# A pipelined transformer block on one core: a new slot table for the feed-forward tiles, and projections on two PSUM banks

## The chip, the cores and the metric

The kernel runs on 1 core of one Trainium2 chip. The metric is the device time of one execution in microseconds, as the median of several runs. Each run stands alone; nothing is averaged over cores.

## What is computed

The reference takes x (16 x 512 x 256, float32) and computes

```python
x = x + 0.5 * ffn(layernorm(x))
x = x + attn(layernorm(x))
x = x + 0.5 * ffn(layernorm(x))
```

`attn` has 16 heads of 16. Of each row of 512 scores only those at or above the 31st largest stay, the others go to -inf before the softmax:

```python
scores = einsum('bhqd,bhkd->bhqk', Q, K) / sqrt(16)
thresh = top_k(scores, 31)[0][..., -1:]
scores = where(scores < thresh, -inf, scores)
context = einsum('bhqk,bhkd->bhqd', softmax(scores), V)
```

`ffn` is a mixture of 16 attention experts with shared weights of the gate in both uses. The gate gives each token 16 weights rw (normalised logits against sim_matrix, relu, a fall-back to the best two, softmax); q, k and v are sums over the experts of rw times a 256 x 64 projection; then one causal attention with head size 64, and an output projection of each expert weighted by rw again.

## The kernel before

All arithmetic is float32. The work is cut into tiles of 128 tokens, 64 in all, 4 to a batch of 512. Two jobs walk over the tiles: job b is the first feed-forward layer (load of x, layer norm, gate, experts, attention, y, second layer norm, xnT), job a is the output projection of the attention and then the second feed-forward layer, with the store. Between them stands the big attention: for each batch 64 units (16 heads x 4 tiles of queries), each 128 queries x 512 keys.

**The order is written by hand, as a table of slots.** A batch has SPAN = 64 slots. For every slot each engine's program issues what the tables name, in order of slots; nothing else schedules. A unit of the attention takes one slot: the scores of a quad of four units (SC, slot 4c + 2, L482), their eviction from PSUM into the ring S of 16 units (EV, 4c + 3, ACT L705), the search of pairs of units by MAX8 and MATCH_REPLACE8 (TOP, 2p + 4, VectorE L812, L814), the threshold as a bias (NBI, POOL L945), ReLU (ACT L716), subtraction (SUB, POOL L950), Exp (ACT L721), transposes (TR, L514), eviction (PTE, L711), PV (L538), and a transpose and copy into ctxr (CT, CTT, CTX). A search of a pair is 14 instructions; it is the work of VectorE.

**The feed-forward tiles** have a slot for every step in AT["a"] and AT["b"], one tile every TILE = 16 slots. Attention of batch n has slots 64n on; job b works ahead of it and job a behind it. Steps named later: x_sum, x_mean, x_sq, x_rstd, h, hT, h_rinv, lg (the front: layer norm, transpose, logits of the gate), shift, top, pair, repl, gate, gate_exp, gate_em, gate_sum, rw, rwT, rw_st (the 16 gate rows, stored to rows_a or rows_b in DRAM), hs (four chunks of four experts: rows are read back, spread over 128 partitions into RB, and POOL multiplies, HS = hT x RB, L909; TensorE then adds the group into pQ, L497), qkv, qkT, sc, sc_max, sc_nmax, sc_exp, sc_rec, sc_norm, pT, attT (the causal attention), rb2 and mix (L927, attT times gate rows), y (L442 and L446, output projection in two halves, then the residual). Job a begins with ctx_rec (VectorE L781), ctx_norm (POOL L851) and ctxT (TensorE L376, left by ACT L617).

**Banks.** Each job has one PSUM bank F (pFa, pFb). Every fill waits until the fill before it has been read (`read`), counted by `fill()` from the table FILLS. The six projections Q0, K0, V0, V1, Q1, K1 of a batch (L466, L473) fill bank b; ACT leaves them to QT, KT and Vst, and VMOVE copies Vst into V. HS and RB have two buffers each and are shared by the jobs; RB2 and mixT have one.

**Queues.** SyncE issues all DMAs in slot order and waits before each for what it needs: x_ld, rw_st, four loads of RB, two of RB2, out. The weights of the attention come in `late_loads()` within the slots of tile 0.

Jobs and attention share VectorE, ACT, POOL and TensorE, so an engine that waits in one step holds up all that stands behind it in the table. `earlier()` and `due()` work out from the tables how many events lie before a slot:

```python
def due(w, j, slot, period, total):
    if (j - slot) % period:
        return None
    k, c = SPAN // period, (j - slot) // period
```

Of the kernel before, what the change touches and what calls it, by code (L numbers as in the profile page):

```python
# [5 lines left out]
F32 = mybir.dt.float32  # L6
# [38 lines left out]
    "a": {k: v - 2 * TILE for k, v in {  # L45
        "ctx_rec": 69, "ctx_norm": 71, "ctxT": 72, "x": 74, "x_mean": 75, "x_sq": 76, "x_rstd": 77, "h": 78,
        "hT": 79, "h_rinv": 79, "lg": 81, "shift": 82, "top": 83, "pair": 84, "repl": 85, "gate": 87,
        "gate_exp": 88, "gate_em": 89, "gate_sum": 90, "rw": 91, "rwT": 92, "rw_st": 93, "hs": 96, "qkv": 104,
        "qkT": 105, "sc": 107, "sc_max": 107, "sc_nmax": 109, "sc_exp": 110, "sc_rec": 111, "sc_norm": 112,
        "pT": 114, "rb2": 110, "attT": 116, "mix": 117, "y": 119, "out": 120,  # L50
    }.items()},
    "b": {k: v - SPAN for k, v in {
        "x_ld": -51, "x_sum": -48, "x_mean": -47, "x_sq": -46, "x_rstd": -45, "h": -44, "hT": -43, "h_rinv": -43,
        "lg": -41, "shift": -40, "top": -39, "pair": -38, "repl": -37, "gate": -34, "gate_exp": -33,
        "gate_em": -32, "gate_sum": -31, "rw": -30, "rwT": -29, "rw_st": -28, "hs": -24, "qkv": -16, "qkT": -15,
        "sc": -14, "sc_max": -13, "sc_nmax": -11, "sc_exp": -10, "sc_rec": -9, "sc_norm": -8, "pT": -6,
        "rb2": -10, "attT": -4, "mix": -3, "y": 0, "y_mean": 2, "y_sq": 3, "y_rstd": 4, "y_norm": 5, "xn": 8,
# [941 lines left out]
```

## Time and profile before

| | us |
|---|---|
| median of 3 runs (4930.96 to 4932.72) | 4932.21 |
| the profiled execution, its own time | 4928.01 |
| its span, first to last instruction | 4926.2 |
| busy: VectorE 92%, TensorE 81%, POOL 75%, ACT 69% | 4551.2, 4014.7, 3710.7, 3383.5 |
| granted TensorE clock, mean over the span | 0.915 of 2.4 GHz |

A "busy" share is taken over the whole span and over stages with different limits. The matmuls' ends are modelled, so busy TensorE is not TensorE at its peak. The durations of single instructions overlap by some tenths of a microsecond when they run back to back, so the distance from start to start is shorter than the duration.

### The profile page before, as it was taken

What the parts mean: (1) busy time and instruction counts of PE and PEld (TensorE: products, weight loads), DVE (VectorE), ACT (ScalarE), POOL (GpSimd) and SP (SyncE); (2) the same over time, 40 slices, a digit from 0 to 9 for tenths busy, and PEclk for the clock granted to TensorE, in tenths of its full rate; (3) what the DMA queues carried; (4) which work ended last, traced back from release to release, by engine and by line L of the source; (5) the groups of instructions that cost most, each with busy time, mean ns of one, the idle gap of its engine ahead of it and who ended that gap; (6) DMA issues with size and microseconds to landing.
All of it is one profiled execution on the core that took longest, in us unless ns stands there. A gap on an engine that the chain in (4) does not pass through costs nothing.

```text
span 4926.2 us, 111637 instructions
## 1 busy us (share of the span) xinstructions
PE 4014.7 (81%) x29004; PEld 3302.3 (67%) x29004; DVE 4551.2 (92%) x10838; ACT 3383.5 (69%) x8261; POOL 3710.7 (75%) x5070
## 2 busy tenths in 40 slices
PE   5667888888888889888888888888888888877767
PEld 4556677676777667677766766776777777765555
DVE  0299999999999999999999999999999999999980
ACT  2366777777777777777777777777777777766562
POOL 5556787888788787878878787887878788865554
PEclk8887999999999999999999999999999999998788
DMA  3210121211112121211111111211112111111011
GB/s 83 51 28 26 46 53 48 53 47 51 49 49 52 46 53 48 52 47 52 49 48 52 47 53 48 51 48 48 53 46 53 48 51 49 49 37 27 20 28 49
DMA packets 244125, 232.19 MB, mean 47 GB/s; under 512 B 27123, under 2 KB 176628, under 8 KB 243316
## 3 DMA queue, kind: packets, MB, share of 16 engines
q1 hardware_dynamic: 243444, 224.49, 17.2%
q8 instruction: 260, 4.26, 0.4%
q14 instruction: 421, 3.45, 0.3%
HBM read 214.98 MB, written 9.44 MB: 46 GB/s over the span
## 4 chain that ended last, share of the span: by engine, by line
issue 35%; POOL 35%; PE 17%; DVE 9%; ACT 2%; POOLq 1%; DVEq 0%; SPq 0%; DMA 0%; ACTq 0%
POOL HS L909 14%; POOL S L950 7%; PE pQ L497 6%; DVE M L812 6%; POOL mixT L927 4%; DVE W L814 3%; PE pFa L442 2%; PE pFa L446 1%; PE pFb L466 1%; PE pST L482 1%; PE pST L514 1%; PE pFa L384 1%; PE pO L538 1%; PE pFa L386 1%; POOL rstdy L843 1%
## 5 line engine op out<-in xcount | busy, mean ns | idle before, releaser
L497 PE MATMUL pQ<-wf_sb,HS 128*128 128x192 f32 x8192 | 1672.5, 365 | 518.1 <-POOL HS L909 517.6
L812 DVE MAX8 M<-W 128x8 f32<-128x512 f32 x3072 | 1964.5, 682 | 0.0
L497 PEld LDWEIGHTS pQ<-wf_sb,HS 128*128 128x128 f32 x8192 | 1536.4, 215 | 601.3 <-POOL HS L909 462.5
L814 DVE MATCH_REPLACE8 W<-M,W 128x512 f32<-128x512 f32 x2048 | 1370.5, 678 | 0.0
L950 POOL TENSOR_TENSOR S<-S,RL 128x512 f32<-128x512 f32 x1024 | 1306.1, 1277 | 0.0
L716 ACT ACTIVATE RL<-S,NBI 128x512 f32<-128x512 f32 x1024 | 762.0, 744 | 385.5 <-POOL S L950 383.4
L945 POOL TENSOR_TENSOR NBI<-M,edge 128x4 f32<-128x4 f32 x512 | 101.9, 199 | 879.6 <-DVE M L812 849.7
L721 ACT ACTIVATE S<-S,NBI 128x512 f32<-128x512 f32 x1024 | 747.8, 730 | 2.1 <-POOL S L950 2.1
L814 DVE MATCH_REPLACE8 W<-M,S 128x512 f32<-128x512 f32 x1024 | 685.1, 677 | 0.0
L705 ACT COPY S<-pST 128x512 f32<-128x512 f32 x1024 | 525.0, 599 | 223.4 <-PE pST L482 223.4
L812 DVE MAX8 M<-S 128x8 f32<-128x512 f32 x1024 | 652.3, 679 | 27.8 <-issue 26.9
L909 POOL TENSOR_TENSOR HS<-hT_b,RB 128x1024 f32<-128x1024 f32 x256 | 605.3, 2365 | 32.6 <-DMA RB<-rows_b 25.7
L909 POOL TENSOR_TENSOR HS<-hT_a,RB 128x1024 f32<-128x1024 f32 x256 | 606.2, 2368 | 12.6 <-DMA RB<-rows_a 8.6
L711 ACT COPY PTs<-pST 128x512 f32<-128x512 f32 x1024 | 526.4, 607 | 17.6 <-PE pST L514 16.6
L514 PE MATMUL pST<-ident,S 128*128 128x128 f32 x4096 | 506.3, 278 | 10.6 <-ACT S L705 10.6
L514 PEld LDWEIGHTS pST<-ident,S 128*128 128x128 f32 x4096 | 474.0, 145 | 27.3 <-ACT S L705 12.5
L538 PEld LDWEIGHTS pO<-PTs,V 128*32 128x32 f32 x8192 | 213.7, 112 | 212.0 <-issue 199.9
L482 PE MATMUL pST<-KT,QT 32*128 32x512 f32 x2048 | 308.1, 673 | 11.0 <-ACT PTs L711 11.0
L538 PE MATMUL pO<-PTs,V 128*32 128x128 f32 x8192 | 284.6, 281 | 8.0 <-ACT ctxr L733 6.2
L442 PE MATMUL pFa<-wof_sb,mixT 128*128 128x256 f32 x512 | 141.8, 425 | 84.9 <-POOL mixT L927 84.9
L442 PEld LDWEIGHTS pFa<-wof_sb,mixT 128*128 128x128 f32 x512 | 101.0, 207 | 115.0 <-issue 80.0
L794 DVE TENSOR_REDUCE mxr_b<-Sr_b 128x1 f32<-128x128 f32 (+1 forms) x64 | 30.1, 470 | 152.5 <-ACT Sr_b L648 152.5
(219 smaller groups left out, 5517.8 us busy)
## 6 DMA issues: line engine op xcount, KB each, us to landing
RB<-rows_b SPq DMA_DIRECT2D x384, 256.0 KB, 3.3
RB<-rows_a SPq DMA_DIRECT2D x384, 256.0 KB, 3.3
x_b<-in_x SPq DMA_DIRECT2D x64, 128.0 KB, 2.8
out_y<-y SPq DMA_DIRECT2D x64, 128.0 KB, 1.7
wf_sb<-in_wf SPq DMA_DIRECT2D x4, 768.0 KB, 7.2
rows_b<-rwT_b SPq DMA_DIRECT2D x64, 8.0 KB, 1.3
wof_sb<-in_wof SPq DMA_DIRECT2D x1, 1024.0 KB, 7.3
rows_a<-rwT_a SPq DMA_DIRECT2D x64, 8.0 KB, 1.4
```

The costliest lines, as they stand in the source:

```text
L482: nc.tensor.matmul(pST[h][:], QT[r:r + 32, g // 2, g % 2, m * P:(m + 1) * P], KT[r:r + 32, g // 2, :], start=True, stop=True).then_inc(s_s ...
L497: mm = nc.tensor.matmul(pQ[:, 0:QKV], HS[:, k % 2, e, i, :], wf_sb[:, i, at:at + QKV], start=k + e + i == 0, stop=(k, e, i) == (3, 3, 1))
L514: mm = nc.tensor.transpose(pST[h][:, k * P:(k + 1) * P], S[:, (4 * c + h) % RING, k * P:(k + 1) * P], ident[:])
L538: mm = nc.tensor.matmul(pO[32 * h:32 * h + 32, 0:P], V[:, k, HG * g + h, :], PTs[:, h, k * P:(k + 1) * P], start=k == 0, stop=k == TPB - 1)
L705: nc.scalar.copy(S[:, (4 * c + h) % RING, :], pST[h][:]).then_inc(s_ev, 1)
L711: nc.scalar.copy(PTs[:, h, :], pST[h][:]).then_inc(s_pe, 1)
L716: nc.scalar.activation(RL[:, c % 2, :], S[:, c % RING, :], ACT.Relu, bias=NBI[:, c % RING, 1:2], scale=-STEEP).then_inc(s_rl, 1)
L721: nc.scalar.activation(S[:, c % RING, :], S[:, c % RING, :], ACT.Exp, bias=NBI[:, c % RING, 0:1], scale=HD ** -0.5).then_inc(s_ex, 1)
L812: nc.vector.max(m, src[i]).then_inc(s_tk, 1)
L814: nc.vector.match_replace(W[:, i, :], m, src[i], -BIG).then_inc(s_tk, 1)
L909: nc.gpsimd.tensor_tensor(HS[:, k % 2, :, :, :], J.hT[:, c % 2, :].rearrange("p (k t) -> p k t", k=KC).unsqueeze(1).broadcast_to([P, 4, KC ...
L950: nc.gpsimd.tensor_tensor(S[:, c % RING, :], S[:, c % RING, :], RL[:, c % 2, :], ALU.subtract).then_inc(s_sub, 1)
```

## The change

The table AT is new for both jobs (some 70 numbers). The slots of the attention (SC to CTX), SPAN, TILE and the period of the chunks of hs (2) stay. Of the projections Q0, V0 and Q1 stay in bank b, K0, V1 and K1 go to bank a. The gate rows have four places in DRAM for each job instead of two. The load of wof_sb goes up to the first loads, and the other late loads are issued after the fourth row load of tile 0, not the second. Scores wait for both of their projections, VMOVE for both V. The lines of the kernel shift by up to 9.

```diff
 AT = {
-    "a": {k: v - 2 * TILE for k, v in {
-        "ctx_rec": 69, "ctx_norm": 71, "ctxT": 72, "x": 74, "x_mean": 75, "x_sq": 76, "x_rstd": 77, "h": 78,
...
+    "a": {
+        "ctx_rec": 32, "ctx_norm": 33, "ctxT": 33, "x": 36, "x_mean": 36, "x_sq": 37, "x_rstd": 38, "h": 39,
...
-PROJ = {"Q0": 57 - SPAN, "K0": 59 - SPAN, "V0": 61 - SPAN, "V1": 62 - SPAN, "Q1": 68 - SPAN, "K1": 70 - SPAN}
-VMOVE = 7
+PBANK = {"Q0": "b", "K0": "a", "V0": "b", "V1": "a", "Q1": "b", "K1": "a"}
+PROJ = {"Q0": -2, "K0": -2, "V0": 6, "V1": 7, "Q1": 9, "K1": 6}
+VMOVE = 8
...
-    "a": {k: (AT["a"][k], TILE, TILES) for k in ("ctxT", "x", "hT", "lg", "rwT", "qkT", "sc", "pT", "attT", "y")},
+    "a": {k: (AT["a"][k], TILE, TILES) for k in ("ctxT", "x", "hT", "lg", "rwT", "qkT", "sc", "pT", "attT", "y")}
+    | {k: (s, SPAN, NB) for k, s in PROJ.items() if PBANK[k] == "a"},
     "b": {k: (AT["b"][k], TILE, TILES) for k in ("hT", "lg", "rwT", "qkT", "sc", "pT", "attT", "y", "xn")}
-    | {k: (s, SPAN, NB) for k, s in PROJ.items()},
+    | {k: (s, SPAN, NB) for k, s in PROJ.items() if PBANK[k] == "b"},
 }
...
-                self.rows = nc.dram_tensor(f"rows_{n}", (2, E, P), F32, kind="Internal").ap()
+                self.rows = nc.dram_tensor(f"rows_{n}", (TPB, E, P), F32, kind="Internal").ap()
...
+            sp.dma_start(wof_sb[:], wof).then_inc(s_ld_wof, 16)
...
             def late_loads():
-                sp.dma_start(wof_sb[:], wof).then_inc(s_ld_wof, 16)
...
-                    if not (isinstance(t, int) and t < 2):
-                        held(sp, s_mix, earlier(w, j + J.at["mix"] - J.at["rw_st"] - 2 * TILE, MIXES.values()) + 1)
-                    sp.dma_start(J.rows[c % 2], J.rwT[:]).then_inc(q["rw_st"], 16)
+                    if not (isinstance(t, int) and t < TPB):
+                        held(sp, s_mix, earlier(w, j + J.at["mix"] - J.at["rw_st"] - SPAN, MIXES.values()) + 1)
+                    sp.dma_start(J.rows[c % TPB], J.rwT[:]).then_inc(q["rw_st"], 16)
...
-                        if k == 1 and isinstance(t, int) and (J.n, t) == ("b", 0):
+                        if k == 3 and isinstance(t, int) and (J.n, t) == ("b", 0):
                             late_loads()
...
             def project(w, j):
-                q, F = jobs["b"].sem, jobs["b"].F
                 for c in range(2):
                     for i, key in enumerate((f"Q{c}", f"K{c}")):
                         if not at_proj(key, w, j):
                             continue
-                        wait(pe, q["read"], fill("b", w, j))
+                        J = jobs[PBANK[key]]
+                        wait(pe, J.sem["read"], fill(J.n, w, j))
                         for k in range(KC):
-                            mm = nc.tensor.matmul(F[:], wqk_sb[:, i * KC + k, c * P:(c + 1) * P], xnT[:, k, :],
+                            mm = nc.tensor.matmul(J.F[:], wqk_sb[:, i * KC + k, c * P:(c + 1) * P], xnT[:, k, :],
                                                   start=k == 0, stop=k == KC - 1)
-                        mm.then_inc(q["full"], 1)
+                        mm.then_inc(J.sem["full"], 1)
...
                     if c % QUADS in (0, 2):
-                        key = "K0" if c % QUADS == 0 else "K1"
-                        sl = PROJ[key] - SC - (c % QUADS) * 4 + j
-                        pe.wait_ge(jobs["b"].sem["read"], fill("b", w, sl) + 1)
+                        for key in ("Q0", "K0") if c % QUADS == 0 else ("Q1", "K1"):
+                            J = jobs[PBANK[key]]
+                            sl = PROJ[key] - SC - (c % QUADS) * 4 + j
+                            pe.wait_ge(J.sem["read"], fill(J.n, w, sl) + 1)
...
                     if due(w, j, VMOVE + 4 * g, SPAN, NB):
+                        for key in ("V0", "V1") if g == 0 else ():
+                            J = jobs[PBANK[key]]
+                            act.wait_ge(J.sem["read"], fill(J.n, w, PROJ[key] - VMOVE + j) + 1)
```

**How instructions move.** Job a's first steps in the loop, TensorE, before: the piece around ctxT (pFa<-ident,ctxn), with y's second half ahead of it and the transposes TR behind.

```order
L446 MATMUL pFa<-wof_sb,mixT 128x256 x4
L448 MATMUL pFa<-x_a,ident 128x256
L399 MATMUL pFb<-simn,hT_b 128x16 x2
L497 MATMUL pQ<-wf_sb,HS 128x192 x8
L376 MATMUL pFa<-ident,ctxn 128x128 x2
L455 MATMUL pFb<-ident,xn 128x128 x2
L514 MATMUL pST<-ident,S 128x128 x16
L520 MATMUL pO<-ident,cT 128x128
```

The same place in the change:

```order
L517 MATMUL pST<-ident,S 128x128 x16
L523 MATMUL pO<-ident,cT 128x128
L378 MATMUL pFa<-ident,ctxn 128x128 x2
L401 MATMUL pFb<-simn,hT_b 128x16 x2
L500 MATMUL pQ<-wf_sb,HS 128x192 x8
L408 MATMUL pFa<-ident,rw_a 16x128
L414 MATMUL pFb<-ident,qk_b 64x128 x2
L485 MATMUL pST<-KT,QT 128x512 x4
```

ctxT stands now right behind TR and ahead of the logits, the first group and the scores of slot 2; ctx_rec and ctx_norm, for which it waits, are one slot before it and in the same slot.

TensorE ahead of the scores of slot 6 (pST<-KT,QT), the slots in which the projections of the batch lie, before:

```order
L432 MATMUL pFa<-PTf_a,v_a 128x128 x4
L466 MATMUL pFb<-xnT,wqk_sb 128x512 x2
L514 MATMUL pST<-ident,S 128x128 x16
L520 MATMUL pO<-ident,cT 128x128
L393 MATMUL pFb<-ident,h_b 128x128 x2
L497 MATMUL pQ<-wf_sb,HS 128x192 x8
L442 MATMUL pFa<-wof_sb,mixT 128x256 x4
L466 MATMUL pFb<-xnT,wqk_sb 128x512 x2
L482 MATMUL pST<-KT,QT 128x512 x4
```

and in the change:

```order
L434 MATMUL pFa<-PTf_a,v_a 128x128 x4
L448 MATMUL pFb<-wof_sb,mixT 128x256 x4
L450 MATMUL pFb<-x_b,ident 128x256
L500 MATMUL pQ<-wf_sb,HS 128x192 x8
L476 MATMUL pFb<-wv_sb,xnT 128x256 x4
L468 MATMUL pFa<-xnT,wqk_sb 128x512 x2
L485 MATMUL pST<-KT,QT 128x512 x4
L542 MATMUL pO<-PTs,V 32x128 x16
```

Both have K1 (the last wqk_sb row) right before the scores; the change has V0 there too, y of job b whole in the slots before, and one more expert group since the scores of slot 2.

POOL in the start, from the first HS of a tile of job b on, before:

```order
L909 TENSOR_TENSOR HS<-hT_b,RB 128x1024
L878 COPY mr_b<-v_b 128x2
L909 TENSOR_TENSOR HS<-hT_b,RB 128x1024 x2
L927 TENSOR_TENSOR mixT<-attT_b,RB 128x1024
L883 TENSOR_TENSOR fb_b<-R_b,L_b 128x16
L884 TENSOR_SCALAR na_b<-v_b 128x1
L885 TENSOR_SCALAR pos_b<-L_b 128x16
L886 TENSOR_SCALAR RL_b<-L_b 128x16
L887 TENSOR_SCALAR nv_b<-v_b 128x1
L889 TENSOR_SCALAR fb_b<-fb_b,na_b 128x16
L891 TENSOR_TENSOR mk_b<-fb_b,pos_b 128x16
L909 TENSOR_TENSOR HS<-hT_b,RB 128x1024
```

and in the change:

```order
L918 TENSOR_TENSOR HS<-hT_b,RB 128x1024
L869 TENSOR_SCALAR mn_b<-sm_b 128x1
L918 TENSOR_TENSOR HS<-hT_b,RB 128x1024 x2
L850 TENSOR_SCALAR ve_b<-vs_b 128x1
L852 TENSOR_TENSOR rstd_b<-ve_b,minus_half 128x1
L875 TENSOR_SCALAR nmr_b<-mn_b,rstd_b 128x1
L850 TENSOR_SCALAR sg_b<-ss_b 128x1
L852 TENSOR_TENSOR rinv_b<-sg_b,minus_half 128x1
L936 TENSOR_TENSOR mixT<-attT_b,RB 128x1024
```

The mix of the tile before, and the gate (fb_b to mk_b), stood between the third and the fourth HS; both stand behind the fourth now. The piece of the change begins with the second HS.

## Rows read from the trace of the kernel before

**Rows 1.** Page, part 2: VectorE's busy tenths in 40 slices of 123 us

```profile
DVE  0299999999999999999999999999999999999980
```

**Rows 2.** Instructions that touch M, VectorE, whole run; then idle before them, by releaser

```profile
L812 DVE MAX8 M<-W x3072: 662/682/706, 226.7 to 4789.3; 128x8 f32<-128x512 f32 x192
...
L812 DVE MAX8 M<-S x1024: 627/678/701, 224.2 to 4781.7; 128x8 f32<-128x512 f32 x171
...
  issue: 26.9, 11
```

**Rows 3.** Chain that ended last, from 60 to 150 us: start us, us, what

```profile
61.63 2.35 POOL HS L909
...
127.33 2.35 POOL HS L909
...
139.57 2.35 POOL mixT L927
...
143.85 2.31 POOL HS L909
```

**Rows 4.** The same chain, the last 110 us

```profile
4819.61 2.32 POOL HS L909
...
4853.02 2.35 POOL HS L909
...
4882.25 2.35 POOL HS L909
```

**Rows 5.** Timeline, POOL, 0 to 30 us: start us, us, engine, line, operation [idle before]

```profile
16.95 0.22 POOL L895 TENSOR_TENSOR em_b<-eg_b,mk_b 128x16 f32<-128x16 f32 x1 [0.42 <-ACT eg_b L578]
...
24.63 2.34 POOL L909 TENSOR_TENSOR HS<-hT_b,RB 128x1024 f32<-128x1024 f32 x1 [0.78 <-DMA RB<-rows_b]
```

**Rows 6.** Timeline, SyncE's queue, the late loads; then page, part 6, one transfer

```profile
22.14 0.42 SPq L288 DMA_DIRECT2D wof_sb<-in_wof  x1
...
39.14 0.81 SPq L300 DMA_DIRECT2D bv_col<-in_bv  x2
...
wof_sb<-in_wof SPq DMA_DIRECT2D x1, 1024.0 KB, 7.3
```

**Rows 7.** Timeline, TensorE, 2500 to 2575 us, middle of the run

```profile
2504.44 0.33 PE L406 MATMUL pFb<-ident,rw_b 128*16 128x128 f32 x1 [3.69 <-POOL rw_b L901]
2504.57 4.50 PE L497 MATMUL pQ<-wf_sb,HS 128*128 128x192 f32 x16
...
2517.02 1.99 PE L442 MATMUL pFa<-wof_sb,mixT 128*128 128x256 f32 x8 [0.67 <-POOL mixT L927]
2518.85 1.88 PE L466 MATMUL pFb<-xnT,wqk_sb 128*128 128x512 f32 x4
2520.66 1.14 PE L482 MATMUL pST<-KT,QT 32*128 32x512 f32 x8
...
2530.56 2.77 PE L497 MATMUL pQ<-wf_sb,HS 128*128 128x192 f32 x16
...
2535.45 0.38 PE L426 MATMUL pFb<-ident,Sr_b 128*128 128x128 f32 x2
...
2570.17 0.91 PE L418 MATMUL pFb<-kT_b,qT_b 64*128 64x384 f32 x2
```

**Rows 8.** Timeline, POOL, 2500 to 2530 us

```profile
2503.26 0.58 POOL L899 TENSOR_TENSOR rgs_b<-gs_b,minus_one 128x1 f32<-128x1 f32 x1
...
2504.54 1.27 POOL L950 TENSOR_TENSOR S<-S,RL 128x512 f32<-128x512 f32 x1
...
2523.14 0.63 POOL L851 TENSOR_TENSOR ctxn<-ctxr,crec 128x256 f32<-128x256 f32 x1
...
2526.17 0.20 POOL L945 TENSOR_TENSOR NBI<-M,edge 128x4 f32<-128x4 f32 x1
```

**Rows 9.** Timeline, ScalarE, 2521 to 2525 us: four evictions, then a ReLU

```profile
2521.82 2.05 ACT L705 COPY S<-pST 128x512 f32<-128x512 f32 x4 [0.36 <-PE pST L482]
2523.73 0.76 ACT L716 ACTIVATE RL<-S,NBI 128x512 f32<-128x512 f32 x1
```

More of the change, by code:

```diff
@@ L44 @@
 AT = {
-    "a": {k: v - 2 * TILE for k, v in {
-        "ctx_rec": 69, "ctx_norm": 71, "ctxT": 72, "x": 74, "x_mean": 75, "x_sq": 76, "x_rstd": 77, "h": 78,
[L47 to L57, printed above, removed]
+    "a": {
+        "ctx_rec": 32, "ctx_norm": 33, "ctxT": 33, "x": 36, "x_mean": 36, "x_sq": 37, "x_rstd": 38, "h": 39,
+        "hT": 40, "h_rinv": 40, "lg": 41, "shift": 42, "top": 42, "pair": 43, "repl": 44, "gate": 45,
+        "gate_exp": 46, "gate_em": 47, "gate_sum": 48, "rw": 49, "rwT": 50, "rw_st": 51, "hs": 64, "qkv": 72,
+        "qkT": 74, "sc": 75, "sc_max": 76, "sc_nmax": 78, "sc_exp": 79, "sc_rec": 81, "sc_norm": 81, "rb2": 81,
+        "pT": 83, "attT": 85, "mix": 88, "y": 93, "out": 94,
+    },
@@ new lines @@
+    "b": {k: v - 2 * SPAN for k, v in {
+        "x_ld": 7, "x_sum": 10, "x_mean": 12, "x_sq": 13, "x_rstd": 15, "h": 15, "hT": 16, "h_rinv": 16, "lg": 17,
+        "shift": 18, "top": 18, "pair": 19, "repl": 20, "gate": 21, "gate_exp": 22, "gate_em": 23, "gate_sum": 24,
+        "rw": 25, "rwT": 26, "rw_st": 27, "hs": 40, "qkv": 48, "qkT": 50, "sc": 51, "sc_max": 52, "sc_nmax": 54,
+        "sc_exp": 55, "sc_rec": 57, "sc_norm": 57, "rb2": 57, "pT": 59, "attT": 61, "mix": 64, "y": 69,
+        "y_mean": 70, "y_sq": 71, "y_rstd": 72, "y_norm": 73, "xn": 76,
@@ L330, in ffn @@
                     held(sp, s_mix, earlier(w, j, MIXES.values()))
-                    pairs = J.rows[c % 2].rearrange("(c o) t -> o c t", o=2)
+                    pairs = J.rows[c % TPB].rearrange("(c o) t -> o c t", o=2)
                     for o in range(2):
@@ L675, in leave_projection @@
             def leave_projection(w, j):
[L676 to L677 removed]
                 for c in range(2):
                     if at_proj(f"Q{c}", w, j):
[L680 to L683 removed]
+                        J = jobs[PBANK[f"Q{c}"]]
+                        act.wait_ge(J.sem["full"], fill(J.n, w, j) + 1)
+                        nc.scalar.activation(QT[:, c, 0, :], J.F[:], ACT.Identity, scale=keep[:, 0:1], bias=bias[:, c, 0, 0:1])
+                        nc.scalar.activation(QT[:, c, 1, :], J.F[:], ACT.Identity, scale=keep[:, 1:2], bias=bias[:, c, 1, 0:1]
+                                             ).then_inc(J.sem["read"], 1)
                     if at_proj(f"K{c}", w, j):
[L685 to L686 removed]
+                        J = jobs[PBANK[f"K{c}"]]
+                        act.wait_ge(J.sem["full"], fill(J.n, w, j) + 1)
+                        nc.scalar.activation(KT[:, c, :], J.F[:], ACT.Identity, bias=kbias[:, c:c + 1]
+                                             ).then_inc(J.sem["read"], 1)
                     if at_proj(f"V{c}", w, j):
[L688 to L690 removed]
+                        J = jobs[PBANK[f"V{c}"]]
+                        act.wait_ge(J.sem["full"], fill(J.n, w, j) + 1)
+                        nc.scalar.copy(Vst[:, 2 * c:2 * c + 2, :], J.F[:].rearrange("p (n m) -> p n m", n=2)
+                                       ).then_inc(J.sem["read"], 1)
             def slot(w, j):
```

20 lines of the change are left out of this document (5 added, 15 removed).

## The prediction

> **What bounds the kernel now.** I read the busy shares in 40 slices first: the reader is to see a VectorE that is almost idle in the first two slices, at 9 tenths in all others, and idle again at the end [rows 1]. The instructions that write M then give the ends of that middle: the first top-k search starts at 224.2 us and the last at 4789.3 (done at 4790.4), and of the time before them only 26.9 us is idle, in 11 pieces of "issue", one for each jump back of the loop [rows 2]. So 512 pairs of rows take 4566 us, 8.9 us a pair, and the kernel is three sums: **a start of 224.2 us, 4566 us of VectorE without a gap, and an end of 135.8 us** (4926.2 less 4790.4). The profiled execution took 4928.0 us, 1.8 more than its span and 4.2 less than the median of 4932.2; I work out differences and add them to the median. About 0.2%, 10 us, is what a measurement of this kernel can tell from no change.
>
> What bounds start and end is the feed-forward layer of one tile. The chain of waits of the start has the first expert product HS of tiles 1 and 3 at 61.6 and 127.3 us, 33 us a tile, and the mix of the tile before sits between the third and fourth product [rows 3]. In the end the same product of the last three tiles is at 4819.6, 4853.0 and 4882.3 [rows 4].
>
> **The start.** All work of the tiles stays; what moves is who waits. (a) The gate chain of tile 1 now ends before the first HS of tile 0. That HS stood at 24.6 us; the gate of tile 0 ended at 17.2 [rows 5]. Tile 1's chain has the same operations and no start-up before it; I give it 10 to 11 us more, so HS starts at about 28.3. (b) SyncE issues the late weight loads, 22.1 to 39.95 us now [rows 6], behind the fourth row load of tile 0 instead of the second. That load follows the row store of tile 1, which needs the first expert group on TensorE (up to twice 2.77 us at half clock, about 5.4), so the loads run from about 37.7 to 55.2, and the row load of tile 1 (3.3 to landing by the page, 3.4 with the wake-up) lets HS of tile 1 start at 58.7, 3 us sooner than now. Moving the 1 MB of wof_sb ahead costs nothing: it lies under the two fronts; without that cover it would cost its 7.3 us to landing [rows 6]. (c) One period: HS 2.35 [rows 3], then the y variance, the gate row and the score reciprocal 3.0, HS 2.3, a mean 0.2, HS 2.3 makes 10.2; the fourth HS waits for rows that are requested only after the next tile's store (about 9.0 after the first HS) and start at 12.4, end at 14.8; its group on TensorE 2.8; leave, transpose, scores 4.6; the two halves of y and the residual 4.2; the copy, the gate exponential and its mask 1.8. Sum 28.2 against 33 [rows 3]. HS of tile 5 is then at 58.7 + 4 x 28.2 = 171.5. From there the four products, both first projections (3.65 more on TensorE), the q/k/v leave and the first scores take 23.8, so the search starts at 195.3. **Gain 29 us** (bounds 15 to 45: half the gain of a period, and the fourth HS not waiting).
>
> **The end.** Walking the same way from the end of the search: HS of tiles 61, 62, 63 at 26.5, 56.3 and 76.0 after it, against 29.2, 62.6 and 91.9 now [rows 4]; tile 63 has no front behind it and its gate rows lie ready, so its period is 20. Its last mix starts at 104.8, and from there to the end it is 11.0 as now (4915.2 to 4926.2). That makes 115.8 against 135.8. **Gain 20 us** (bounds 10 to 28).
>
> **The middle.** Here nothing can be gained, as VectorE has no gap but the loop's, and something can be lost. VectorE needs the scores of a quad evicted (EV, L705) every 17.8 us. Before, the scores stood 5 us and more ahead: those of slot 6 started at 2520.66 and the search that reads them at 2526, when POOL's next NBI was released [rows 7, 8]. Three chains close on that now; they come once in a batch, about the projections, in batches 1 to 14 (job a is absent in batch 0, job b in 15).
>
> First, ctx_rec, ctx_norm and ctxT now stand in neighbouring slots (32, 33, 33 instead of 37, 39, 40). TensorE stands at ctxT until VectorE has ended the search of slot 0 and POOL has normalised (ctxn, 0.6) [rows 8]. From there to the scores of slot 2: 0.2 + 0.6, ctxT and logits 0.7, one group 2.7, two transposes 0.35, in all 4.55. From those scores through the group of slot 5: the stretch 2520.66 to 2535.45, 14.8 us, holds scores, PV, y's second half, two groups, x and one TR [rows 7]; take off logits and three transposes (1.0), add y's first half 1.85, the masked scores 1.05, pT 0.4, attT 0.9: 17.95. V0 and K1 now stand before the scores of slot 6: 2 x 1.82 = 3.65 (K from 2518.85 to 2520.66 [rows 7]). K1's leave 0.75 and the first eviction 0.55 follow. Sum 27.45, while VectorE wants the row after three pairs, 26.6. **0.85 us lost even at full clock.** TensorE was idle for 5 to 7 us before ctxT. Row: after 3.7 us idle, a group took 4.50 instead of 2.77 [rows 7], though other groups after such gaps did not. I take that 1.7, so 2.55 in all.
>
> The Trainium skill ("TensorE: Matmul & The Clock Gate", section "HAM oscillation — how this bites in real kernels") says that a wait of this kind before every burst makes every burst begin at half clock, again and again, not sometimes. By that rule the group after each ctxT would be slow as a whole (5.4), 1 us more in each batch, 4953 in place of 4939.
>
> Second, slots 7 to 11, from the start E of the late eviction: four evictions 1.9 and a ReLU 0.65 [rows 9], SUB 1.3 [rows 8], the wait for h to 4.4, reciprocal 0.9, mix 2.35 and HS 2.35, y variance 1.3, SUB 1.25, rw 1.1, reciprocal 0.55: 14.1. Then on ACT the norm, y_norm and logits 1.2, Q1's leave 1.35, ReLU and Exp 1.25, small ones 0.85, first eviction 0.55: E + 19.3, where VectorE is ready at E + 18.1. **1.2 us lost.** Cover gone here: Q1's leave used to lie in slot 4.
>
> Third, Q0 and K0 (3.65 on TensorE, 2.0 on ACT) stand in slot 62 before that slot's scores; ACT then evicts at the last moment and reaches the ctxr copy 0 to 0.95 us after VectorE's ctx_rec is ready for it. I take 0.25.
>
> Sum 4.0 us a batch (bounds 2.0, full clock and no third loss, to 5.0), 14 batches: **56 us lost** (28 to 70). In the 40 or so other tile pairs the same chains end 1.0 to 1.5 us before VectorE needs them; cost nothing, covered by that slack alone. The second bank and the four row places cost no time of their own: the extra waits of the scores (four reads for two) and of VMOVE are for copies long done, and the row store's wait on mix is for a tile four back.
>
> **Sum**: -29 - 20 + 56 = +7, so 4939 us.
>
> **Rivals.**
> (1) *The middle holds.* The chains are within 1 to 3 us of harmless; if TensorE keeps its clock over the gap and my serial sums are 1 us long each, the losses are 0 to 1 us a batch: -49 + 0..14, some 4890. For: sums of single rows tend to be long, since waits overlap. Against: 0.85 remains with every operation at its fastest.
> (2) *The slack of the other tiles is gone too* (slower). Mechanism: ctxT in slot 33 leaves TensorE low-clocked in every tile, not once a batch; with the wide tiles' copies (up to 0.3 us more each) the eviction comes 1 us late in the 42 other pairs. From a slack under 1.0 it decides: 4939 + 42 = 4981. For: in the profile of before TensorE is already 81% busy. Against: groups after gaps of 3 us are often at 2.87.
> (3) *The edges give half*: the fourth HS waits longer for its rows behind store and x load on SyncE's queue, and the end is bound by TensorE at low clock; 25 us less gain, 4964.
> That the change does nothing is no case: the order moves on every engine.
>
> **Chances.** Forecast 0.50 (own range 4915 to 4962), rival 1 0.27, rival 2 0.15, rival 3 0.08. The range 4880 to 4985 takes in rivals 1 and 2 and leaves about 1 in 5 out. Faster by over 0.2%: 0.27 + a fifth of 0.50, 0.37. Same: a bit over a third of 0.50, 0.18. Slower: the rest, 0.45. Both signs hold much of the chance, as two sums of about 50 us stand against each other.
>
> **What would show it.** First M<-S near 195 (now 224.2); end 116 after the last search; "M<-S" with idle before it from "ACT S" of some 50 us in about 28 pieces, and crec with waits on ctxr below 14 us; group times after ctxT of 4.5. VectorE's middle longer than 4566 by 56. I am wrong if the middle stays at 4566, if the search starts after 210, or if the idle pieces are more than 50.

## The result, and the profile after

The changed kernel takes **5007.78 us** (median of 4 runs, 5001.98 to 5024.97) against 4932.32 before: ratio 1.0159 (95% interval 1.0134 to 1.0184). It is slower by 75 us, on the side to which 0.45 of the chances went, but 23 us above the top of the range. The profiled execution took 5024.97, the slowest of the four, with a span of 5023.0; the others spread over 7 us, where those of before spread over 2.

I cut the span into the same three sums, and the middle's idle time by its releaser:

| | start | middle | end | VectorE idle in the middle | of it at the turns |
|---|---|---|---|---|---|
| before | 224.2 | 4566 | 136 | 26.9 | 26.9 |
| forecast of the change | 195 | 4622 | 116 | 83 | 27 |
| the change | 201.8 | 4687 | 134.5 | 138.6 | 52.3 |

Instructions that touch M, VectorE, whole run of the changed kernel; these answer to [rows 2]:

```profile
L821 DVE MAX8 M<-W x3072: 662/681/712, 204.3 to 4887.4; 128x8 f32<-128x512 f32 x192
...
L821 DVE MAX8 M<-S x1024: 627/677/708, 201.8 to 4879.9; 128x8 f32<-128x512 f32 x171
```

Waits of VectorE between 202 and 4888 us, changed kernel (us in total, times, longest):

```profile
DVE M L821 <- ACT S L711: 80.0, 56, 3.1
DVE M L821 <- issue: 52.3, 11, 5.1
DVE crec L790 <- ACT ctxr L739: 7.4, 9, 0.9
```

Before there was only the "issue" line, 26.9 in 11. (Both kernels have one more wait, of about 1 us, at the first search itself, which is not counted.) Where the pieces lie is seen in one batch of the timeline (VectorE; idle time in brackets). The first row is the turn of the loop, at slot 0; a pair of searches takes two slots and 8.9 us, so the others are the searches of slots 8, 12, 20, 28 and 32 and the reciprocal of slot 32:

```profile
2533.17 1.29 DVE L821 MAX8 M<-S 128x8 f32<-128x512 f32 x2 [4.65 <-issue]
...
2571.45 1.29 DVE L821 MAX8 M<-S 128x8 f32<-128x512 f32 x2 [2.68 <-ACT S L711]
...
2590.93 1.29 DVE L821 MAX8 M<-S 128x8 f32<-128x512 f32 x2 [1.88 <-ACT S L711]
...
2627.35 1.29 DVE L821 MAX8 M<-S 128x8 f32<-128x512 f32 x2 [0.97 <-ACT S L711]
...
2663.53 1.29 DVE L821 MAX8 M<-S 128x8 f32<-128x512 f32 x2 [0.57 <-ACT S L711]
...
2682.05 1.29 DVE L821 MAX8 M<-S 128x8 f32<-128x512 f32 x2 [0.53 <-ACT S L711]
...
2691.71 0.26 DVE L790 RECIPROCAL crec<-ctxr 128x16 f32<-128x16 f32 x1 [0.85 <-ACT ctxr L739]
```

Summed over the run: slot 8, 37.9 us in 14 pieces, one in each of batches 1 to 14; slot 12, 23.6 in 13; slots 20, 28 and 32 together 14.6 in 22, in seven or eight batches of the loop only; the reciprocal 7.4 in 9, seven of them in slot 32 and two in slot 0; 2.7 in six smaller pieces; the turns 52.3 in 11, against 26.9. That is 111.7 more than before, of the 120.5 by which the middle grew in this execution. The other 9 are not idle time: VectorE is busy for 4547.4 us of the middle against 4539.0 before, with the same searches.

**Slot 8.** TensorE of the same batch, from ctxT (which the kernel before reaches without any idle time) to the scores of slot 6:

```profile
2542.89 0.69 PE L378 MATMUL pFa<-ident,ctxn 128*128 128x128 f32 x2 [5.99 <-POOL ctxn L860]
...
2544.08 4.11 PE L500 MATMUL pQ<-wf_sb,HS 128*128 128x192 f32 x16
...
2548.45 1.14 PE L485 MATMUL pST<-KT,QT 32*128 32x512 f32 x8
...
2563.42 2.76 PE L500 MATMUL pQ<-wf_sb,HS 128*128 128x192 f32 x16
2566.02 1.89 PE L476 MATMUL pFb<-wv_sb,xnT 128*128 128x256 f32 x8
2567.75 1.88 PE L468 MATMUL pFa<-xnT,wqk_sb 128*128 128x512 f32 x4
2569.56 1.14 PE L485 MATMUL pST<-KT,QT 32*128 32x512 f32 x8
```

It stands 5.99 us at ctxT; from there to 2570.6 it has no idle row, the group behind ctxT takes 4.11 us instead of 2.77, and V0 and K1 come last. The scores start at 2569.56, when VectorE had been free since 2568.77.

**Slot 12.** The same batch, POOL, ScalarE and TensorE in order of time:

```profile
2576.22 2.39 POOL L936 TENSOR_TENSOR mixT<-attT_a,RB 128x1024 f32<-128x1024 f32 x1
...
2578.57 2.35 POOL L918 TENSOR_TENSOR HS<-hT_b,RB 128x1024 f32<-128x1024 f32 x1
...
2582.31 1.27 POOL L959 TENSOR_TENSOR S<-S,RL 128x512 f32<-128x512 f32 x1
...
2584.63 0.57 POOL L929 TENSOR_TENSOR rrs_b<-rs_b,minus_one 128x1 f32<-128x1 f32 x1
...
2585.24 0.51 ACT L597 ACTIVATE Sr_b<-Sr_b,rrs_b 128x256 f32<-128x256 f32 x1 [2.99 <-POOL rrs_b L929]
...
2586.14 0.25 ACT L636 ACTIVATE Lr_a<-pFa,rinv_a 128x16 f32<-128x16 f32 x1
...
2586.54 0.38 PE L414 MATMUL pFa<-ident,qk_a 128*64 128x128 f32 x2 [2.50 <-ACT Lr_a L636]
...
2588.09 2.09 PE L485 MATMUL pST<-KT,QT 32*128 32x512 f32 x8
```

POOL's mix and HS stand one behind the other; ScalarE waits 2.99 us for the reciprocal behind them, Lr is read after that, TensorE waits 2.50 us for Lr's bank, and its scores then take 2.09 us instead of 1.14.

**Start.** Chain of the start, from 85 to 122 us (start, us, what):

```profile
85.95 2.31 POOL HS L918
...
108.77 3.78 PE pFb L444 x8
112.55 1.99 PE pFb L448 x8
...
115.10 0.48 ACT x1r L671 x2
...
116.15 0.76 POOL HS L918
```

The first HS of tiles 1, 2, 3, 4 and 5 start at 54.45, 85.9, 116.1, 147.1 and 177.2, 30.7 us a tile. y and its residual take 6.3 us (108.77 to 115.03), at a granted clock of 0.65 between 108 and 115.

**End.** Timeline of the last tile but none, all engines:

```profile
4973.19 3.47 PE L444 MATMUL pFa<-wof_sb,mixT 128*128 128x256 f32 x8 [0.57 <-ACT Sr_a L652]
...
4974.21 2.35 POOL L918 TENSOR_TENSOR HS<-hT_a,RB 128x1024 f32<-128x1024 f32 x1
...
4978.86 2.76 PE L500 MATMUL pQ<-wf_sb,HS 128*128 128x192 f32 x16
...
4979.59 0.34 SPq L340 DMA_DIRECT2D out_y<-y  x1
...
4980.11 0.82 SPq L324 DMA_DIRECT2D RB<-rows_a  x2
...
4983.66 4.64 POOL L918 TENSOR_TENSOR HS<-hT_a,RB 128x1024 f32<-128x1024 f32 x2 [2.92 <-DMA RB<-rows_a]
```

The group of the first HS stands behind y of the tile before, which runs at a granted clock of 0.70 (4973.2 to 4978.9); SyncE cannot request the next rows before that y is read and stored, so the second HS comes 9.45 us behind the first.

### The profile page after: what moved, and what is told of

Read it like the earlier page. It is cut to its first block, busy times and chain, and to the rows that moved or that the text cites. A ratio compares the mean times of both kernels' runs of the same rounds, so it can differ in the third digit from the quotient of the medians.

```text
span 5023.0 us, 111712 instructions
## 1 busy us (share of the span) xinstructions
PE 4030.5 (80%) x29004; PEld 3327.5 (66%) x29004; DVE 4559.1 (91%) x10838; ACT 3338.3 (66%) x8261; POOL 3711.3 (74%) x5070
## 4 chain that ended last, share of the span: by engine, by line
issue 34%; PE 27%; POOL 20%; DVE 12%; ACT 4%; DVEq 2%; POOLq 1%; SPq 0%; ACTq 0%; DMA 0%
PE pQ L500 11%; DVE M L821 7%; POOL HS L918 6%; POOL S L959 5%; DVE W L823 4%; POOL mixT L936 3%; PE pST L485 3%; ACT S L711 1%; DVEq L243 1%; PE pFb L444 1%; PE pO L542 1%; PE pST L517 1%; PE pFb L448 1%; PE pFa L386 1%; PE pFb L401 1%
## 5 line engine op out<-in xcount | busy, mean ns | idle before, releaser
L500 PE MATMUL pQ<-wf_sb,HS 128*128 128x192 f32 x8192 | 1648.2, 361 | 222.9 <-POOL HS L918 222.8
L517 PE MATMUL pST<-ident,S 128*128 128x128 f32 x4096 | 518.7, 282 | 78.4 <-ACT S L711 49.2
L517 PEld LDWEIGHTS pST<-ident,S 128*128 128x128 f32 x4096 | 481.0, 147 | 90.7 <-ACT S L711 51.1
L378 PE MATMUL pFa<-ident,ctxn 128*128 128x128 f32 x128 | 40.2, 415 | 398.5 <-POOL ctxn L860 398.5
L542 PE MATMUL pO<-PTs,V 128*32 128x128 f32 x8192 | 294.7, 288 | 0.0
L378 PEld LDWEIGHTS pFa<-ident,ctxn 128*128 128x128 f32 x128 | 17.6, 194 | 414.4 <-issue 357.1
L597 ACT ACTIVATE Sr_a<-Sr_a,rrs_a 128x128 f32<-128x128 f32 (+1 forms) x64 | 36.0, 562 | 275.5 <-POOL rrs_a L929 275.5
L954 POOL TENSOR_TENSOR NBI<-M,edge 128x4 f32<-128x4 f32 x512 | 102.1, 199 | 155.5 <-DVE M L821 109.8
## 6 DMA issues: line engine op xcount, KB each, us to landing
x_b<-in_x SPq DMA_DIRECT2D x64, 128.0 KB, 2.0
out_y<-y SPq DMA_DIRECT2D x64, 128.0 KB, 1.7
```

What stands on the lines that cost most here:

```text
L500: mm = nc.tensor.matmul(pQ[:, 0:QKV], HS[:, k % 2, e, i, :], wf_sb[:, i, at:at + QKV], start=k + e + i == 0, stop=(k, e, i) == (3, 3, 1))
L517: mm = nc.tensor.transpose(pST[h][:, k * P:(k + 1) * P], S[:, (4 * c + h) % RING, k * P:(k + 1) * P], ident[:])
L542: mm = nc.tensor.matmul(pO[32 * h:32 * h + 32, 0:P], V[:, k, HG * g + h, :], PTs[:, h, k * P:(k + 1) * P], start=k == 0, stop=k == TPB - 1)
```

## The experiments

Theory 1 after the result: three steps of the middle each hold the next scores, ctxT in slot 33 first of all, and each can be taken out by moving that step. The rival for each is that the cover is gone everywhere, so that the wait comes back at the next place. before_pad16 starts from the kernel before, all others from the changed one, and a time stands against the kernel before on the same chip.

| kernel | start | middle | end | idle | turns | us, ratio to before |
|---|---|---|---|---|---|---|
| b_new | 201.3 | 4639.8 | 133.7 | 94.9 | 23.9 | 4970.2, 1.0081 (1.0065 to 1.0098) |
| a_new | 214.2 | 4765.3 | 137.4 | 210.8 | 37.2 | 5110.6, 1.0366 (1.0349 to 1.0384) |
| spread | 202.4 | 4656.5 | 137.7 | 109.1 | 51.2 | 4997.3, 1.0137 (1.0121 to 1.0154) |
| ctx_later | 201.6 | 4609.0 | 137.4 | 65.8 | 39.6 | 4947.8, 1.0035 (1.0023 to 1.0046) |
| b_new_max | 202.0 | 4568.3 | 133.5 | 28.1 | 25.0 | 4906.8, 0.9952 (0.9936 to 0.9969) |
| ctx_later_q1 | 204.7 | 4624.3 | 137.5 | 79.8 | 39.7 | 4954.7, 1.0047 (1.0030 to 1.0064) |
| pad16 | 203.9 | 4659.1 | 135.0 | 109.8 | 34.4 | 5000.0, one run |
| loads_early | 208.4 | 4684.7 | 135.3 | 137.2 | 51.1 | 5030.4, one run |
| before_pad16 | 223.9 | 4567.5 | 134.3 | 28.5 | 28.5 | 4927.5, one run |
| pad48 | 205.6 | 4659.1 | 136.8 | 109.9 | 36.6 | 5003.4, one run |
| out_later | 198.3 | 4672.4 | 130.2 | 126.0 | 50.0 | 5002.8, one run |
| ctx_gate | 205.4 | 4903.0 | 138.7 | 352.4 | 25.3 | 5249.0, one run |
| norm_later | 204.2 | 4579.8 | 135.7 | 39.8 | 39.8 | 4919.3, 0.9971 (0.9959 to 0.9984) |
| pad16_pool | 202.9 | 4677.0 | 136.9 | 129.7 | 51.7 | 5018.8, one run |
| norm_out_pad | 201.1 | 4570.2 | 128.0 | 28.9 | 27.3 | 4903.2, 0.9945 (0.9928 to 0.9961) |

The eleventh turn of ctx_later and of ctx_later_q1 (3.9 us each) is put down to ScalarE's S and is not in their column of turns. Start, middle, end and idle time are those of the profiled execution; that of ctx_later_q1 took 4968.4, 14 more than the next.

### The two halves of the table

```diff
 b_new: AT["a"] of before, rb2 of job a three slots later; PROJ:
+PBANK = {"Q0": "b", "K0": "a", "V0": "b", "V1": "b", "Q1": "b", "K1": "a"}
+PROJ = {"Q0": -2, "K0": -2, "V0": 6, "V1": 7, "Q1": 9, "K1": 5}
 a_new: AT["b"] of before, rb2 of job b three slots later; PROJ and VMOVE of before, all in bank b
```

> Job b's new slots with job a's old ones; projections Q0, V0, V1, Q1 in bank b, K0 and K1 (slot 5) in bank a. Theory 1 (the middle's loss comes from job a's ctxT in slot 33, which holds TensorE ahead of the scores, together with V0 and K1 in slot 6): the search of slot 8 waits under 1 us a batch instead of 2.7; the search of slot 12 still waits 1.9 (Q1 in slot 9 and b's front chain). Search starts at 202 us, end 136 after the last search; about 4932 - 22 + 14 x 2 = 4938, and 25 more if the loop's turns stay at 4.7 us. Rival (the loss comes from b's table and the projections alone): slot 8 still waits 2.7, turns 4.7, about 4995.

> Job a's new slots with job b's old ones and the old projections. Theory 1: ctxT in slot 33 without V0 and K1 in slot 6 leaves about 1 us of the wait before the search of slot 8 and none before slot 12, since Q1 is in slot 4; start 224, end 135; 4932 + 0 to 20. Rival (b's table makes the loss): no idle time of VectorE but the loop's turns, 4932 within 5. If the turns are 4.7 us here too, 25 more in both.

b_new has no wait before any search; what it has is this (waits of VectorE, 210 to 4800 us):

```profile
DVE mxr_a L803 <- ACT Sr_a L652: 71.0, 53, 5.1
DVE M L821 <- issue: 23.9, 11, 2.3
```

So b's table with the projections in slots 5, 6, 7 and 9 makes neither the wait of slot 8 nor that of slot 12, and the turns are 2.2 us. Its time, 4970, is still 32 above the 4938 expected. Its start has the whole gain. But a_new, which has b's old table and shares with b_new the later weight loads, starts its search at 214.2 too, 10 us before the kernel before: its first HS of tile 1 is at 49.42 where that of the kernel before is at 61.63, and its period is still 33.1 us. So some 10 of the 22 us of the start come without b's new table, by the rows through the later loads (SyncE issues them behind the fourth row load there too); they were not put back alone with the old table. The wait that b_new has instead I had not expected in either theory: sc_max of job a stands in the slot of its own scores, as it did before. a_new fails both theories. It loses 161 us before the reciprocal of ctx_rec:

```profile
DVE crec L790 <- ACT ctxr L739: 160.7, 55, 4.6
```

ctx_rec is in slot 32, and ScalarE copies the last ctxr in slot 33; in this mixture ScalarE mostly comes there 3 to 4 us after VectorE. The new step is tight even without the new b.

### b_new with one step moved

```diff
-        "sc": 107, "sc_max": 107
+        "sc": 107, "sc_max": 108
```

> b_new with VectorE's row maximum of job a (sc_max) one slot later, behind the next search. Theory 1: the 70 us in which VectorE waited for the scores copy Sr_a go, since it comes one search (8.9 us) later; nothing else held VectorE but the turns (2.2 us each). Start 201, middle 4570, end 134: 4907. Rival (TensorE is late as a whole and the wait moves to the evictions): idle of 50 us or more before the searches, about 4965.

4906.8, as theory 1 said to the microsecond; the 71 us are gone and nothing took their place (waits of VectorE, 210 to 4768 us):

```profile
DVE M L821 <- issue: 25.0, 11, 3.2
DVE M L821 <- ACT S L711: 3.1, 8, 0.4
```

It beats both kernels: it takes the new start and keeps the old middle. Job a has its old table in it, so it does not say which of a's new steps does the harm; that is what the next runs are for.

### ctxT

```diff
 spread: V1, K1 to bank b
-PROJ = {"Q0": -2, "K0": -2, "V0": 6, "V1": 7, "Q1": 9, "K1": 6}
-VMOVE = 8
+PROJ = {"Q0": -2, "K0": -2, "V0": 6, "V1": 8, "Q1": 9, "K1": 7}
+VMOVE = 9
 ctx_later: spread, and for job a
-"ctxT": 33, "pT": 83, "attT": 85
+"ctxT": 35, "pT": 86, "attT": 87
 ctx_gate: b_new_max, and for job a, with K1 in slot 8 of bank b
-"ctx_rec": 69, "ctx_norm": 71, "ctxT": 72
+"ctx_rec": 68, "ctx_norm": 69, "ctxT": 69
```

> The changed kernel with one projection a slot: V0 6, K1 7, V1 8, Q1 9, all but K0 in bank b, V moved in slot 9. Theory 1: the search of slot 8 loses K1's 1.8 us of its wait (2.7 to about 0.9); the search of slot 12 keeps 1.9 or gains. About 5007 - 25 = 4982. Rival (TensorE is held by ctxT and the cold clock alone, order of projections does not count): 5007 within 10.

> As spread, and ctxT in slot 35 behind the scores of slot 34, pT in slot 38 and attT in slot 39 of each tile of job a (mod 16: 3, 6, 7; mix stays at 8). Theory 1: TensorE no longer stands at ctxT ahead of the scores; the waits before the searches of slots 8, 20, 28 and 32 go (4.2 us a batch and more); left are slot 12 (1.9) and the turns: about 4932 - 22 + 27 + 25 = 4962. Rival: the idle pieces stay as they are in spread.

> The table of b_new_max with one part of the change put in by itself: ctx_rec in slot 36, ctx_norm and ctxT in 37, so that TensorE stands at ctxT, right ahead of the scores of slot 38, until VectorE has ended the search of slot 36 (as in the changed kernel for 32, 33 and 34); K1 goes to slot 8 of bank b for it. Theory 1: idle time of 1 to 3 us comes before the search of slot 8 in each batch, and some in the other tiles: 25 to 60 us more than b_new_max's 4907, mean 4945. Rival: TensorE's wait is covered, 4907 within 8.

spread takes 1.5 us off each wait of slot 8 (16.0 us in 13 pieces, 1.23 each) and 0.5 off slot 12, but the time fell by 10 us where 25 were expected: pieces of about 0.5 us came before the searches of slots 36 (6.9 us in 12) and 52 (5.4 in 12). So half of what left slots 8 and 12 came back elsewhere. ctx_later ends the wait of slot 8 but for 3.5 us in three pieces, those of slots 20, 32, 36 and 52 and part of the reciprocal's, and takes 50 us off the time, 14 more than expected; slot 12 keeps 8.2 us in six pieces. pT and attT of job a moved with ctxT in it, and its turns are some 8 us less in all, for which I have no reason. ctx_gate is the same kind of step put into a table that had next to no waits: 342 us slower, nine times the 38 that I wrote (waits of VectorE, 210 to 5100 us; then what ctxT waited for, TensorE, whole run, its weight loads counted in; the matmuls alone waited 412.7 us, 63 times):

```profile
DVE M L821 <- ACT S L711: 327.0, 114, 4.9
```

```profile
L378 PE MATMUL pFa<-ident,ctxn x128: 273/422/477, 355.8 to 5151.0; 128*128 128x128 f32 x128
...
  POOL ctxn L860: 486.3, 75
```

The direction is shown, and VectorE's waits and TensorE's standing come with it. My size was far off because in that table each of the four tiles of a batch loses twice, before the search behind ctxT (slots 8, 24, 40, 56, up to 4.9 us) and before the one after it (slots 12, 28, 44, 60, up to 4.5). The place is a worse one, too: at 2512.81 us halves of y of both jobs and a group stand between ctxT and the scores, which start 9.5 us behind it; in the batch of the changed kernel shown above they start 5.6 us behind. K1's move was made with it and was not tried alone.

### The wait of slot 12

```diff
 ctx_later_q1: ctx_later, Q1 to bank a
-"Q1": 9
+"Q1": 1
 norm_later: ctx_later (Q1 in 9)
-"sc_norm": 81 (a), "sc_norm": 57 (b)
+"sc_norm": 82 (a), "sc_norm": 58 (b)
```

> ctx_later with Q1 in slot 1, bank a, instead of slot 9. Theory 1: Q1's 1.8 us on TensorE and 1.35 on ScalarE leave the chain of slots 7 to 11, so the wait before the search of slot 12 (8.2 us in all) goes: about 4940. Rival: Q1 right behind the turn and ahead of the scores of slot 2 makes a new wait before slot 4, 4950 or more.

> ctx_later with the scaling of the gate's attention rows (sc_norm, ScalarE) in slots 10 and 2 instead of 9 and 1. Theory Q (the wait before the search of slot 12 comes from POOL: mix and HS of slot 8 one behind the other, 4.7 us, then SUB, the gate row and rrs; ScalarE stands at sc_norm for rrs, and behind it TensorE at the transposes of qk for Lr): Lr no longer stands behind that wait, the 8.2 us of idle time before the search of slot 12 go, 4948 - 8 = 4940. Rival (rw and the score reciprocal hold the next step just as well, by rwT or SUB): still 5 to 10 us there, time within 5 of 4948.

Moving Q1 did not help slot 12: 17.0 us in 12 pieces of 1.4, against 8.2 in six, with the same chain. The time, 4954.7, is what the rival gives, but not by its mechanism: there is no wait before the search of slot 4 behind a turn, and slot 8 has 10.4 us in 12 pieces. The chain (ctx_later_q1, timeline of one batch):

```profile
1680.13 0.51 ACT L597 ACTIVATE Sr_b<-Sr_b,rrs_b 128x256 f32<-128x256 f32 x1 [2.30 <-POOL rrs_b L929]
...
1681.43 0.61 PE L414 MATMUL pFa<-ident,qk_a 128*64 128x128 f32 x2 [2.70 <-ACT Lr_a L636]
...
1682.18 2.09 PE L485 MATMUL pST<-KT,QT 32*128 32x512 f32 x8
```

norm_later lets Lr pass the wait for rrs, and every wait of the middle goes, also those at other places (VectorE, 210 to 4780 us):

```profile
DVE M L821 <- issue: 39.8, 11, 3.9
```

That is 28.5 us where 8 were expected: ctx_later's pieces at slots 0, 8, 28, 44, 56 and 60 went with those of slot 12. Which of them hung on sc_norm itself and which only followed from lateness elsewhere was not taken apart.

### Start, end, and the turns

```diff
 loads_early: late_loads() with wof_sb in it, after the second row load (k == 1)
 out_later:
-"y": 93, "out": 94
+"y": 93, "out": 99
 pad16, pad48, before_pad16 (ahead of emit(dve, slot)); pad16_pool (ahead of emit(pool, slot))
+            for _ in range(16):
+                dve.sem_inc(s_pad_dve, 1)
 norm_out_pad: norm_later + out_later + pad16
```

> The changed kernel with the late loads and wof_sb back behind the second row load of tile 0. Forecast of the part on the loads: the start loses 3 us or more of its gain, first search at 205 to 210 instead of 201.8; middle and end as in the changed kernel. Rival: the fourth row load hides behind the other work, start within 1 us.

> The changed kernel with the store of a tile's result (out) in slot 3 behind the four row loads of the next tile, instead of slot 14 between the first and the second. Theory E: in the end SyncE no longer holds the second row load until y is read, so the second HS of the last tile starts some 7 us earlier (9.5 us behind the first before), its TensorE group 4 us; the end falls from 134.5 to about 129. Rival (TensorE's y at half clock ahead of the group sets it alone): end 133 to 135.

> The changed kernel with 16 semaphore increments on VectorE ahead of its loop (a shift of its instructions only). If the length of the idle time at the loop's turns hangs on where the instructions lie, it changes from 4.75 us a turn (to 2.4 at best: 5007 - 26 = 4981). If it comes from what other engines do at that moment, it stays at 4.2 to 5.1.

> The changed kernel with 48 increments instead of the 16 of pad16. Theory P: the turns come out at yet another value between 2.1 and 5 us, not at 4.75 and not of necessity at pad16's 3.1. Rival (16 increments helped by starting the loop later against the other engines): a value at or below 3.1.

> The kernel before with 16 semaphore increments on VectorE ahead of its loop. Theory P (the idle time at the loop's turns hangs on where VectorE's instructions lie): the turns, 2.2 to 2.8 us before, change to 3 to 5 us, and the time rises by 10 to 25 us. Rival (it hangs on what the change makes the other engines do there): the turns stay at 2.2 to 2.8, time within 5 us of 4930 plus some 2 us of a later start.

> The changed kernel with 16 semaphore increments ahead of POOL's loop, none on VectorE. If only the place of VectorE's own instructions counts for its turn, it stays at 4.75 us; if the two engines' turns hang together, it changes as in pad16 (3.1).

> norm_later with the store in slot 3 (as out_later) and 16 increments ahead of VectorE's loop (as pad16). If the parts add up: end 135.7 less 4.3, turns 3.6 to about 2.5 to 3.2 us (5 to 12 us less over 11), start 1 to 2 later: 4919 - 11 = 4908. Rival: padding sets the turns anew in this program, at no lower value: 4915 to 4919.

With the loads back in their old place the first HS of tile 1 starts at 58.88 instead of 54.45, and the search 6.6 us later. Since the start of kernels with the same b table lies between 198.3 and 205.6, only the 4.4 us at the HS are clear of that spread, in one run. out_later brings the second HS of the last tile to 6.5 us behind the first, and the end to 130.2, 4.3 less; the ends of the kernels that keep the store in its place lie between 133.5 and 138.7, and norm_out_pad, with the store moved, has 128.0.

The turns: 16 increments on VectorE bring them from 4.75 to 3.1 us, 48 to 3.3, 16 on POOL leave them at 4.7, and 16 in the kernel before leave its 2.4 at 2.6. So instructions ahead of VectorE's own loop shorten its turns in the changed kernel, and those ahead of POOL's do not. In the kernel before they made no difference, against theory P, and 48 do no more than 16, which does not tell theory P from its rival. Whether it is the place of VectorE's instructions or the time at which its loop starts was not told apart, and each of these runs is a single one. POOL's own idle time at the turn, 1.8 to 2.6 us in the kernel before, is 3.4 to 4.5 in the changed one and still 2.9 to 4.4 in pad16, so VectorE's is not all that grew there. What rule the turns follow, and why b_new has 2.2 and norm_later 3.6, **stays open**. In norm_out_pad the turns are 2.5, and the time is 4903.2, 5 below the sum of the parts. It is the lowest of all, but not clear of b_new_max: the intervals of their ratios overlap (waits of VectorE, 210 to 4768 us; its lines are one further on):

```profile
DVE M L822 <- issue: 27.3, 11, 3.0
DVE M L822 <- ACT S L712: 0.9, 1, 0.9
DVE crec L791 <- ACT ctxr L740: 0.7, 2, 0.5
```

With the shorter turns of pad16 and pad48 the waits before the searches of slots 20, 28 and 32 went altogether (14.6 us in the changed kernel), and pieces of 0.2 to 0.3 us near slots 36 and 52 were left; the reciprocal's waits did not go but moved to slot 0, 9.6 us in 12 in pad16. So the waits of slots 20 to 32 go with long turns, though not in every batch: the last three turns of the changed kernel are 4.2 to 5.1 us, and no such piece follows them.

## Why the prediction was wrong

The three sums and their signs were right; the balance between them was not. Forecast -29 - 20 + 56; the profiled execution has -22 - 1 + 120 (the median some 17 less). **The step that failed is the middle's sum**, which held two terms at nothing: the loop's turns, taken as fixed at 26.9 us, and the other tiles, "covered by that slack alone". The runs show 52.3 us for the turns and 14.6 for the other tiles. The middle's 64 us too little are 25 of the turns, 15 of the other tiles, 9 of VectorE's longer busy time, 7 of the second chain, 4 of the third, 2 of the first and 3 of small pieces. The end failed as well, by 19 us, and the start by 6.5.

- **Start, (a) and (b).** HS of tile 0 at 28.9 against 28.3. The loads gave more than the 3 us I took: HS of tile 1 at 54.45, not 58.7, since SyncE was through with them at 50, not 55.
- **Start, (c).** The period was the mis-sized term: 30.7, not 28.2. I priced "the two halves of y and the residual 4.2"; they took 6.3. That price came from rows at the full clock [rows 7]; in the new order TensorE has only small matmuls with gaps of 0.5 us between them before y, and the granted clock about y is 0.63 to 0.66 in the four tiles looked at, between its two levels of 1.2 and 2.4 GHz (0.5 and 1). Four periods cost 10 us, of which 4 came back by the loads.
- **End.** The path was wrong. "Walking the same way from the end of the search" gave 26.5, 56.3 and 76.0 for the first HS of the last three tiles; they came at 30, 65 and 86, and the last mix at 124 instead of 104.8: 10 us had come by the first HS of the last tile, 9 more came within it. I let the next tile's HS start as soon as its own gate was ready. In the order it is behind y of the tile before three times over: ScalarE's exponential behind y's copy, TensorE's group behind y, SyncE's row load behind the store of y. out_later shows the third at 4.3 us; the first two are read from rows, not tried apart.
- **Middle, first chain.** Right in mechanism and size: 2.55 us a batch forecast, 2.7 measured (37.9 in 14), and from the reciprocal (2541.90) to the search of slot 8 (2571.45) 29.5 us against my 27.45 + 1.7. ctx_later, against spread, shows that it is ctxT (with pT and attT), and ctx_gate that such a step makes waits in another table; spread shows that K1's 1.8 us count in it.
- **Middle, second chain.** 1.2 forecast, 1.8 measured, but the cause was wrong. "Cover gone here: Q1's leave used to lie in slot 4": ctx_later_q1 put it away again and the wait did not go. The wait is ScalarE's for rrs behind POOL's mix and HS in one slot; I had both in the sum and named the wrong one as decisive.
- **Middle, third chain.** 0.25 us in each of 14 batches forecast, nine pieces of 0.8 measured, and seven of them not where I had put them: Q0 and K0 of slot 62 bear on the reciprocal of slot 0, and there were only two. The seven of slot 32 come in the batches that have the waits of slots 20 to 32. Behind a turn of 4.7 us the reciprocal of slot 0 has nothing left to wait for; with the turns of pad16 the waits of slot 0 are there in 12 batches. That the long turn hides them is read from this, not tried.
- **What the sum did not have.** The turns: I took 26.9 us as fixed ("Here nothing can be gained, as VectorE has no gap but the loop's"), and they doubled, 25 us, for a reason that stays open. Then the other tiles: "the same chains end 1.0 to 1.5 us before VectorE needs them" was too kind by as much in 22 cases, 15 us; rival 2, whose 42 pairs would have made 42. And VectorE's busy time, which grew by 9. The turns' 25 us alone are more than the 23 by which the median lies above the range.

**The clock.** In the kernel before, TensorE comes to ctxT without idle time, and the 53 groups behind a ctxT between 590 and 4320 us take 2.76 to 2.87 us, at a granted clock of 1.0:

```profile
2528.05 0.38 PE L376 MATMUL pFa<-ident,ctxn 128*128 128x128 f32 x2
...
2530.56 2.77 PE L497 MATMUL pQ<-wf_sb,HS 128*128 128x192 f32 x16
```

In the changed one all 51 such groups there take 3.97 to 5.47 us, after 3.2 to 7.0 us of standing at ctxT; the clock is 0.5 at the start of each and 0.50 to 0.71 over the whole. I had weighed the page "TensorE: Matmul & The Clock Gate" of the Trainium skill (section "HAM oscillation — how this bites in real kernels"), by which each burst after such a wait begins at half clock, against single rows that did not show it, and took 1.7 us from one slow row. The trace agrees with the page that every group begins at half clock. It does not agree that every group is slow as a whole: that is so for 8 of the 51. Behind the ctxT of slot 1, where it bears on the first chain, the group took 4.06 to 4.54 us in 12 of 14 batches, 1.3 to 1.8 more than 2.77, so my 1.7 was the better price there. By the rule I had written 4953, nearer than 4939 and still 55 short; that it was nearer is luck, since the missing time was elsewhere. No run separates the time of standing at ctxT from the clock behind it. A slow group need not cost anything: b_new_max, where TensorE comes to ctxT without idle time, has only 20 of 52 such groups below 2.95 us, and its middle is within 2 us of that of the kernel before.

## What to carry to other kernels

A table that shortens the two edges is paid in the middle by each step whose operand another engine finishes late: price a moved step not by its own time but by what stands behind it on its in-order engine while it waits, and give it one slot more wherever the producer ends in the slot before. With job b's new table and job a's old one, a move of sc_max by one slot gave 25 us against the kernel before (b_new_max); in the changed table, moves of one to three slots (ctxT, pT and attT, two projections, sc_norm) turned the 75 us lost into 13 gained (norm_later), and the store and the padding brought it to 28. Walk edges as they are issued, with the previous tile's output ahead of the next tile's input on every engine and on the DMA queue, and price TensorE's rows there at the clock that its idle time leaves it.

## What was unexpected of the hardware

The jump at the end of the loop body cost VectorE 2.1 to 5.1 us a turn from one version to another, with the same work on VectorE, and 16 instructions put ahead of the loop moved it from 4.75 to 3.1 in one run. And the changed kernel has two rhythms in one execution: from turn to turn, seven batches in the profile (3 to 9), with the pieces of slots 20 to 32, take 297 us each, batches 11 and 12, without those, 293 and 294; before, each takes 286 to 287. Its four executions spread over 23 us, those of before over 2; that the number of slow batches differs between them is likely, but only one of them has a profile.
